# Row maxima in causal attention: four PSUM banks used as a ring, and another pacing of the maxima

## The chip, the cores and the metric

The kernel runs on one core of one Trainium2 chip. The metric is the device time of one execution in microseconds. Three executions of the kernel before took 4935.09, 4936.78 and 4944.33 us; the median is 4936.78.

## What is computed

The program is a whole network of eight stages: a mixture of experts, attention, the mixture of experts again, a channel mix, a state-space layer and a second channel mix. The change touches the attention alone. Its input has 8 batches of 1024 tokens and 256 features; there are 16 heads of 16 features.

```python
logits = jnp.einsum('bhqd,bhkd->bhqk', q, k) * scale
mask = jnp.tril(jnp.ones((T, T), dtype=x.dtype))
logits = logits + (1.0 - mask)[None, None, :, :] * big_neg
attn = jax.nn.softmax(logits, axis=-1)
out = jnp.einsum('bhqk,bhkd->bhqd', attn, v)
```

The kernel computes the softmax as exp(logit - row maximum) over its sum, so every query needs the maximum over its keys before its exponentials are taken.

## The kernel before, in words

`attention` (from line 1006) works on 32 groups, each of four heads of one batch (`GH` = 4, `GROUPS` = 32). It does two things at once on TensorE (PE).

**Maxima.** For head x and query tile j of 128 queries, `maximum` in the tensor program multiplies the 128 queries by the (j + 1) x 128 keys that they may see, in bf16 parts, into PSUM (line 1277, in matmuls of at most 512 columns). VectorE (DVE) adds the causal mask and takes the row maximum in one instruction (line 1229), which also writes a scratch tile, `masked[u % 2]`, and is followed by a read of its accumulator into `mx`. `TILES_M` orders the 32 tiles of a group from large to small: four of 1024 keys, four of 896, and so on to four of 128. When a group's last tile is done, `negated` makes three bf16 parts of the negated maxima (lines 1236 to 1239), `parts` transposes them on PE (line 1284) into PSUM too, `transposed` copies them out (line 1245), and SyncE (SP) puts them as extra rows under the queries (`maxima` in the sync program), so that the score matmul subtracts the maximum by itself. In the order of uses the transposing matmul of a group comes after the first two tiles of the next group (`PARTS_AT` = 2). A reciprocal of an older group's sums (line 1252) comes after tile 24, the first of 256 keys.

**Scores and values.** `score` (line 1301) multiplies keys by queries for a unit, that is a key tile and up to 512 queries. A group has 12 units of 512, 128, 384, 256, 512, 128, 512, 256, 512, 384, 512 and 512 queries (`ORDER`), cut into slots of up to 512 columns, each in one of three banks `psE`: 38 slots a group (`SHARES`). ScalarE (ACT) takes the exponential (line 1213), GpSimd (POOL) zeroes the masked corner of units on the diagonal (line 1192), and two units later `values` (line 1317) multiplies by the values into `psO`, which ACT copies out twice a group (line 1203).

**PSUM.** `psM` is two buffers of two banks each; use u of the maxima takes buffer u % 2, so PE's matmul for use u waits until DVE is through with use u - 2. `psE` has three banks and `psO` one: eight in all.

**Pacing.** PE runs one stream in program order. After each score slot s, `maxima(s)` issues the tiles from `upto[s]` to `upto[s + 1]`. The planner counts a tile at its columns, (j + 1) x 128, and a slot at its score columns, and lets the maxima run `AHEAD` = 1.3 groups ahead of the scores. The first 1.3 groups' tiles are issued before any score, and the last group's slots have few or none left.

Of the kernel before, what the change touches and what calls it, by code (L numbers as in the profile page):

```python
# [18 lines left out]
P = 128  # L19
B, L, D = 8, 1024, 256  # L20
N_TOK = B * L
LT = L // P
DH = D // P
TILES = N_TOK // P
BANK = 512
# [752 lines left out]
GH = 4  # L778
GROUPS = B * NH // GH
HG = NH // GH  # L780
AUG = 2 * HD
PARTS = 3

QREP = (3, 2, 1)
SK = 6 * HD
# [220 lines left out]
def attention(nc, tag, qs, ks, vs, oT, rdd, consts):  # L1006

    with ExitStack() as ctx:
        a = Pool_(nc, ctx, tag)
        identb = a.sb("identb", [P, P], bf16)  # L1010
        later = a.sb("later", [P, L])
        qst = [a.sb(f"qst{u}", [P, GH, L], bf16) for u in range(HG)]
# [4 lines left out]
        masked = [a.sb(f"masked{k}", [P, L]) for k in range(2)]  # L1017
        mx = [a.sb(f"mx{k}", [P, GH * LT]) for k in range(2)]
        mrest = a.sb("mrest", [P, GH * LT])
        mp = a.sb("mp", [P, PARTS, GH * LT], bf16)  # L1020
        mT = a.sb("mT", [PARTS * GH * LT, P], bf16)
# [3 lines left out]
        rden = [a.sb(f"rden{u}", [GH * LT, P]) for u in range(2)]  # L1025
        rd = [a.sb(f"rd{u}", [P, L]) for u in range(2)]
        on = [a.sb(f"on{u}", [P, L]) for u in range(2)]
        psM = [a.ps(f"psM{k}", [P, 2 * BANK]) for k in range(2)]
        NE = 3
        psE = [a.ps(f"psE{k}", [P, BANK]) for k in range(NE)]  # L1030
        psO = a.ps("psO", [P, BANK])
# [2 lines left out]
        m_ready, m_used, mp_ready, m_loaded = (a.sem(n) for n in ("m_ready", "m_used", "mp_ready", "m_loaded"))  # L1034
# [8 lines left out]
        UNITS = [(kt, max(h * BANK, kt * P), (h + 1) * BANK) for h, kt in ORDER]  # L1043
# [20 lines left out]
        uses.update({use_of_parts(g): (g, N_M) for g in range(GROUPS)})  # L1064
        N_USES = len(uses)

        AHEAD = 1.3
        SLOTS = [(n, x, c) for n in range(NU) for x, c in SHARES[n]]
        per_group = sum(GH * (q1 - q0) for _, q0, q1 in UNITS)
        upto, done, k, work = [], 0, 0, 0  # L1070

        def cost(u):
            return (TILES_M[uses[u][1]][1] + 1) * P if uses[u][1] < N_M else 0

        for s in range(-1, GROUPS * NS_):
            if s >= 0:
                n, _, c = SLOTS[s % NS_]
                done += c * (UNITS[n][2] - UNITS[n][1])
            while k < N_USES and work + cost(k) <= done + AHEAD * per_group:
                work += cost(k)  # L1080
                k += 1
            upto.append(k)
# [8 lines left out]
        with nc.Block() as block:  # L1091
# [128 lines left out]
            @block.vector  # L1220
            def _(dve):
                link = Link(dve, d_step)
                dve.wait_ge(consts_loaded, 32)

                def maximum(g, k, u):
                    x, j = TILES_M[k]
                    w = (j + 1) * P
                    dve.wait_ge(m_ready, u + 1)
                    dve.tensor_tensor_reduce(masked[u % 2][:, 0:w], psM[u % 2][:, 0:w], later[:, L - w:], 1.0, -3e38,  # L1229
                                             ALU.add, ALU.max, mx[g % 2][:, x * LT + j:x * LT + j + 1]).then_inc(m_used, 1)  # L1230

                def negated(g, u):
                    m = mx[g % 2]
                    link.at(3 * g)
                    dve.wait_ge(m_used, u + 1)
                    link.step(dve.tensor_scalar(mp[:, 0, :], m[:, :], -1.0, None, ALU.mult))
                    link.step(dve.scalar_tensor_tensor(mrest[:, :], m[:, :], -1.0, mp[:, 0, :], ALU.mult, ALU.subtract))
                    link.step(dve.tensor_copy(mp[:, 1, :], mrest[:, :]))
                    dve.tensor_tensor(mp[:, 2, :], mrest[:, :], mp[:, 1, :], ALU.subtract).then_inc(mp_ready, 1)

                def transposed(g, u):
                    dve.wait_ge(m_ready, u + 1)
                    if g:
                        dve.wait_ge(m_loaded, 16 * PARTS * g)
                    dve.tensor_copy(mT[:, :], psM[u % 2][0:PARTS * GH * LT, 0:P]).then_inc(m_used, 1)

                def inverse(g):
                    u = g % 2
                    dve.wait_ge(den_loaded[u], 16 * GH * (g // 2 + 1))
                    if g >= 2:  # L1250
                        dve.wait_ge(rden_stored[u], 16 * (g // 2))
                    dve.reciprocal(rden[u][:, :], den[u][:, :]).then_inc(r_ready, 1)

                for u in range(N_USES):
                    g, k = uses[u]
                    if k < N_M:
                        maximum(g, k, u)
                        if k == N_M - 1:
                            negated(g, u)
                        if k == INV_AT and g >= 2:  # L1260
                            inverse(g - 2)
                    else:
                        transposed(g, u)
                inverse(GROUPS - 2)
                inverse(GROUPS - 1)

            @block.tensor
            def _(pe):
                def maximum(g, k, u):
                    x, j = TILES_M[k]  # L1270
                    if k == 0:
                        pe.wait_ge(loaded[g % HG], LOADS * (g // HG + 1))
                    if u >= 2:
                        pe.wait_ge(m_used, u - 1)
                    for c in range(0, (j + 1) * P, BANK):
                        r = min(BANK, (j + 1) * P - c)
                        ins = pe.matmul(psM[u % 2][:, c:c + r], qst[g % HG][0:SK, x, j * P:(j + 1) * P],  # L1277
                                        kst[g % HG][0:SK, x, c:c + r], start=True, stop=True)
                    ins.then_inc(m_ready, 1)

                def parts(g, u):
                    pe.wait_ge(mp_ready, g + 1)
                    pe.wait_ge(m_used, u - 1)
                    pe.matmul(psM[u % 2][0:PARTS * GH * LT, 0:P], mp[:, :, :].rearrange("p k n -> p (k n)"),
                              identb[:, :], start=True, stop=True).then_inc(m_ready, 1)

                def maxima(s):
                    for u in range(upto[s], upto[s + 1]) if s >= 0 else range(upto[0]):
                        g, k = uses[u]
                        if k < N_M:  # L1290
                            maximum(g, k, u)
                        else:
                            parts(g, u)

                def score(k, i):
                    g, n = k // NU, k % NU
                    (kt, q0, q1), (x0, c), s = UNITS[n], SHARES[n][i], slots_to(k) + i
                    if s >= NE:
                        pe.wait_ge(w_ready, s - NE + 1)
                    for x in range(c):  # L1300
                        ins = pe.matmul(psE[s % NE][:, x * (q1 - q0):(x + 1) * (q1 - q0)],  # L1301
                                        kst[g % HG][0:SK + PARTS, x0 + x, kt * P:(kt + 1) * P],
                                        qst[g % HG][0:SK + PARTS, x0 + x, q0:q1], start=True, stop=True)
                    ins.then_inc(e_ready, 1)
                    maxima(s)

                def values(k):
                    g, n = k // NU, k % NU
                    kt, q0, q1 = UNITS[n]
                    if n in DIAGS:  # L1310
                        pe.wait_ge(sel_ready, sel_count(g, n))
                    else:
                        pe.wait_ge(w_ready, slots_to(k) + len(SHARES[n]))
                    if n in FIRSTS and k:
                        pe.wait_ge(o_copied, 2 * g + FIRSTS.index(n))
                    for x in range(GH):
                        ins = pe.matmul(psO[AUG * x:AUG * (x + 1), q0 % BANK:q0 % BANK + q1 - q0], va[g % HG][:, kt, x, :],  # L1317
                                        wt[k % NW][:, x, 0:q1 - q0], start=(n in FIRSTS), stop=(n in LASTS))
                    ins.then_inc(w_used, 1)

                LOADS = 16 * (2 * sum(QREP) + 1)
                pe.wait_ge(consts_loaded, 32)
                pe.wait_ge(ones_ready, HG + 2)
                maxima(-1)
                for k in range(GROUPS * NU):
                    if k % NU == 0:
                        pe.wait_ge(m_loaded, 16 * PARTS * (k // NU + 1))
                    shares = SHARES[k % NU]
                    early = (k - LAG) % NU not in FIRSTS
                    for i in range(len(shares)):  # L1330
                        score(k, i)
                        if k >= LAG and i == (len(shares) // 2 if early else len(shares) - 1):
                            values(k - LAG)
                for k in range(GROUPS * NU - LAG, GROUPS * NU):
                    values(k)
# [1412 lines left out]
```

## Time and profile before

| | |
|---|---|
| median of three executions | 4936.78 us |
| the profiled execution | 4933.36 us |
| its span | 4931.6 us |
| PE busy in the span | 4195.4 us (85%) |
| DVE busy | 3070.1 us (62%) |
| ACT busy | 2309.5 us (47%) |
| maxima on DVE, line 1229 | 734.0 us in 1024 instructions |
| maxima on PE, line 1277 | 421.8 us in 1536 matmuls |
| scores on PE, line 1301 | 413.7 us in 1536 matmuls |
| exponentials on ACT, line 1213 | 627.4 us in 1216 instructions |

The first maxima matmul starts at 889.9 us of the span and the last at 1867.7. Times in the profile are microseconds, those marked as a mean are nanoseconds. A matmul's duration contains its drain through the array, so durations of consecutive matmuls overlap; it is the distance of two starts that tells how long one holds the engine. The same holds of DVE and ACT. PEld is the weight load of a matmul.

### The profile page before, as it was taken

How to read it: one execution, taken by the hardware profiler on the slowest of the kernel's cores; microseconds unless marked ns; L12 is line 12 of the kernel's file. 1: busy time of each engine (PE TensorE's matmuls, PEld its weight loads, DVE VectorE, ACT ScalarE, POOL GpSimd, SP SyncE). 2: the span in 40 equal slices, each digit the busy share in tenths (PEclk: the TensorE clock that was granted, in tenths of full speed). 3: DMA queues.
4: the chain of work that ended last, by engine and by line, in shares of the span. 5: the costliest groups of instructions: out<-in, count | busy, mean ns of one | idle time of the engine just before them, and what ended most of it. 6: DMA issues, size and time to landing. Idle time of an engine off the chain costs nothing. (4 is left out here: it accounts for less than half of the span.)

```text
span 4931.6 us, 117903 instructions
## 1 busy us (share of the span) xinstructions
PE 4195.4 (85%) x49696; PEld 2649.1 (54%) x49696; DVE 3070.1 (62%) x5364; ACT 2309.5 (47%) x3824; POOL 2409.9 (49%) x1569
## 2 busy tenths in 40 slices
PE   6399968699999996739997799879999999997798
PEld 5255545233333333625555544367777777875576
DVE  4511145687888884641116466479899899997574
ACT  1021124366666663101115367667667776763233
POOL 1034344222222223113432245479999899997553
PEclk6599989799999998769998899989999999998899
DMA  6132256655555544422323236643333333333552
GB/s 214 39 83 44 37 181 225 110 88 88 88 88 88 88 71 158 144 78 46 49 36 102 85 143 259 233 124 98 94 88 100 94 101 88 98 98 105 215 202 80
DMA packets 325609, 548.93 MB, mean 111 GB/s; under 512 B 55104, under 2 KB 221168, under 8 KB 325072
## 3 DMA queue, kind: packets, MB, share of 16 engines
q1 hardware_dynamic: 291328, 487.10, 36.5%
q0 software_dynamic: 24576, 34.10, 4.4%
q10 hardware_dynamic: 9168, 20.09, 1.1%
q8 instruction: 396, 6.49, 0.6%
q14 instruction: 141, 1.16, 0.1%
HBM read 326.98 MB, written 212.86 MB: 109 GB/s over the span
## 5 line engine op out<-in xcount | busy, mean ns | idle before, releaser
L2331 POOL TENSOR_TENSOR s_hc<-s_hs,s_ct 128x1024 f32<-128x1024 f32 x512 | 1213.5, 2384 | 91.6 <-DVE s_hs L2310 77.1
L2310 DVE TENSOR_TENSOR_SCAN s_hs<-s_dA,s_psB 128x1024 f32<-128x1024 f32 x512 | 1167.3, 2285 | 126.3 <-PE s_psB L2244 63.8
L2244 PE MATMUL s_psB<-s_diag,s_duT 128*32 128x128 f32 x32768 | 962.7, 274 | 53.2 <-issue 28.2
L2244 PEld LDWEIGHTS s_psB<-s_diag,s_duT 128*32 128x32 f32 x32768 | 909.6, 111 | 157.5 <-issue 108.4
L1229 DVE CUSTOM_DVE_ANT_0 a_masked<-a_psM,a_later 128x1024 f32<-128x1024 f32 (+7 forms) x1024 | 734.0, 753 | 213.7 <-PE a_psM L1277 201.5
L1213 ACT ACTIVATE a_wt<-a_psE 128x512 f32<-128x512 f32 (+1 forms) x1216 | 627.4, 578 | 356.1 <-PE a_psE L1301 346.5
L2187 ACT ACTIVATE s_dA<-s_dlt,s_aneg 128x1024 f32<-128x1024 f32 x512 | 587.8, 1148 | 343.5 <-DVE s_hs L2310 339.6
L1192 POOL TENSOR_SCALAR_AFFINE_SELECT a_wt<-a_wt 128x512 f32<-128x512 f32 x256 | 162.3, 634 | 769.9 <-ACT a_wt L1213 769.9
L1277 PE MATMUL a_psM<-a_kst,a_qst 96*128 96x512 bf16 (+3 forms) x1536 | 421.8, 337 | 99.9 <-DVE a_mx L1229 68.0
L1301 PE MATMUL a_psE<-a_qst,a_kst 99*128 99x512 bf16 (+3 forms) x1536 | 413.7, 331 | 4.1 <-ACT a_wt L1213 2.4
L2167 ACT ACTIVATE s_diag<-s_ident,s_bt 128x128 f32<-128x128 f32 x972 | 322.2, 388 | 13.6 <-ACT s_ys L2176 13.5
L1317 PE MATMUL a_psO<-a_wt,a_va 128*32 128x512 f32 (+3 forms) x3072 | 328.1, 499 | 0.4 <-POOL a_wt L1192 0.4
L1301 PEld LDWEIGHTS a_psE<-a_qst,a_kst 99*128 99x128 bf16 x1536 | 129.0, 97 | 325.3 <-ACT a_wt L1213 218.3
L1277 PEld LDWEIGHTS a_psM<-a_kst,a_qst 96*128 96x128 bf16 x1536 | 143.4, 98 | 295.9 <-DVE a_mx L1229 203.2
L2257 PE MATMUL s_psY<-s_hc,s_gsum 128*32 128x512 f32 x2064 | 251.6, 597 | 5.9 <-POOL s_hc L2331 5.9
L1991 PE MATMUL s_ps<-s_hT,s_w_in 128*128 128x512 f32 x512 | 224.7, 597 | 1.7 <-ACT s_hT L1794 1.3
L667 POOL DMA_INDIRECT x<-m2f_y,m_slots x64 | 100.8, 1575 | 216.4 <-DVE m2f_y L711 201.8
L667 POOL DMA_INDIRECT x<-m1f_y,m_slots x64 | 100.8, 1575 | 216.1 <-DVE m1f_y L711 201.5
L691 ACT ACTIVATE m2f_mid<-m2f_psU,m2f_bu 128x512 f32<-128x512 f32 x96 | 65.8, 686 | 282.5 <-PE m2f_psU L744 282.5
L691 ACT ACTIVATE m1f_mid<-m1f_psU,m1f_bu 128x512 f32<-128x512 f32 x96 | 65.8, 686 | 282.4 <-PE m1f_psU L744 282.4
L759 PE MATMUL m1f_psD<-m1f_wdn,m1f_mid 128*128 128x256 f32 (+1 forms) x768 | 190.5, 394 | 0.0
L759 PE MATMUL m2f_psD<-m2f_wdn,m2f_mid 128*128 128x256 f32 (+1 forms) x768 | 190.5, 394 | 0.0
(305 smaller groups left out, 5939.4 us busy)
## 6 DMA issues: line engine op xcount, KB each, us to landing
s_dlt<-dd SPq DMA_DIRECT2D x128, 512.0 KB, 4.5
a_qst<-qs SPq DMA_DIRECT2D x192, 128.0 KB, 6.7
a_kst<-ks SPq DMA_DIRECT2D x192, 128.0 KB, 7.2
yd<-s_ys ACTq DMA_DIRECT2D x33, 512.0 KB, 2.7
vs<-a_va SPq DMA_DIRECT2D x8, 2048.0 KB, 6.9
a_va<-vs SPq DMA_DIRECT2D x32, 512.0 KB, 10.4
zsd<-s_zs SPq DMA_DIRECT2D x32, 512.0 KB, 7.5
ucd<-s_uc SPq DMA_DIRECT2D x8, 2048.0 KB, 13.3
```

The source lines that it names most:

```text
L759: ins = pe.matmul(psD[k][:, j * D:(j + 1) * D], mid[u][0:r, f, t * P:(t + 1) * P], wdn[0:r, e, f, :], start=(f == 0), stop=(f == FT - 1))
L1213: act.activation(wt[k % NW][:, x:x + c, 0:q1 - q0], psE[s % NE][:, 0:c * (q1 - q0)].rearrange("p (x q) -> p x q", x=c), ACT.Exp, scale=HD ...
L1229: dve.tensor_tensor_reduce(masked[u % 2][:, 0:w], psM[u % 2][:, 0:w], later[:, L - w:], 1.0, -3e38, ALU.add, ALU.max, mx[g % 2][:, x * LT ...
L1277: ins = pe.matmul(psM[u % 2][:, c:c + r], qst[g % HG][0:SK, x, j * P:(j + 1) * P], kst[g % HG][0:SK, x, c:c + r], start=True, stop=True)
L1301: ins = pe.matmul(psE[s % NE][:, x * (q1 - q0):(x + 1) * (q1 - q0)], kst[g % HG][0:SK + PARTS, x0 + x, kt * P:(kt + 1) * P], qst[g % HG][0 ...
L1317: ins = pe.matmul(psO[AUG * x:AUG * (x + 1), q0 % BANK:q0 % BANK + q1 - q0], va[g % HG][:, kt, x, :], wt[k % NW][:, x, 0:q1 - q0], start=( ...
L2167: ins = act.activation(diag[:, place(n, u), c, :], ident[:, :], ACT.Copy, scale=bt[u][:, c, n:n + 1])
L2187: act.activation(dA[k % 2][:, :], dlt[j % 2][:, q % NB, :], ACT.Exp, scale=aneg[:, k:k + 1]).then_inc(dA_ready, 1)
L2244: ins = pe.matmul(psB[s][DG * m:DG * (m + 1), c * P:(c + 1) * P], duT[j % 2][:, c, DG * r:DG * (r + 1)], diag[:, place(NB * g + m, u), c, ...
L2257: ins = pe.matmul(psY[DG * r:DG * (r + 1), c:c + BANK], gsum[:, :], hc[NB * (g % 2) + r][:, c:c + BANK], start=(g == 0), stop=(g == NQ - 1))
L2310: dve.tensor_tensor_scan(hs[k % 2][:, :], dA[k % 2][:, :], psB[s][:, :], 0.0, ALU.mult, ALU.add).then_inc(scanned, 1)
L2331: pool.tensor_tensor(hc[NB * (g % 2) + r][:, :], hs[k % 2][:, :], ct[:, g, :], ALU.mult).then_inc(weighed, 1)
```

## The change

`psM` becomes one tensor of four banks, and a planner gives each use a place in it: two neighbouring banks, from an even one, for tiles of 640 keys and more (`TILES_M[..][1] * P >= BANK`), one bank for tiles of up to 512 keys and for the transposing matmul. Places go round the four banks. PE's matmul for use u waits for the last earlier use that held any of its banks (`free[u]`). DVE's instruction for use u waits, besides for the matmul, until use u - 2 is done, whose scratch tile it writes over. The pacing counts a tile at its columns plus 76 (`START`), and scales the slots so that a group's slots weigh as much as a group's tiles.

```diff
-        psM = [a.ps(f"psM{k}", [P, 2 * BANK]) for k in range(2)]
+        psM = a.ps("psM", [P, 4 * BANK])
...
+        place, free, holder, at = [], [], [0] * 4, 0
+        for u in range(N_USES):
+            n = 2 if uses[u][1] < N_M and TILES_M[uses[u][1]][1] * P >= BANK else 1
+            at = (at + n - 1) // n * n % 4
+            place.append(at * BANK)
+            free.append(max(holder[at:at + n]))
+            holder[at:at + n] = [u + 1] * n
+            at += n
+
         AHEAD = 1.3
         SLOTS = [(n, x, c) for n in range(NU) for x, c in SHARES[n]]
-        per_group = sum(GH * (q1 - q0) for _, q0, q1 in UNITS)
+
+        START = 76
+        per_group = sum(j * P + P + START for _, j in TILES_M)
+        columns = sum(GH * (q1 - q0) for _, q0, q1 in UNITS)
         upto, done, k, work = [], 0, 0, 0
 
         def cost(u):
-            return (TILES_M[uses[u][1]][1] + 1) * P if uses[u][1] < N_M else 0
+            return (TILES_M[uses[u][1]][1] + 1) * P + START if uses[u][1] < N_M else 0
 
         for s in range(-1, GROUPS * NS_):
             if s >= 0:
                 n, _, c = SLOTS[s % NS_]
-                done += c * (UNITS[n][2] - UNITS[n][1])
+                done += c * (UNITS[n][2] - UNITS[n][1]) * per_group / columns
...
                 def maximum(g, k, u):
                     x, j = TILES_M[k]
                     w = (j + 1) * P
+                    if u >= 2:
+
+                        dve.wait_ge(m_used, u - 1)
                     dve.wait_ge(m_ready, u + 1)
-                    dve.tensor_tensor_reduce(masked[u % 2][:, 0:w], psM[u % 2][:, 0:w], later[:, L - w:], 1.0, -3e38,
+                    dve.tensor_tensor_reduce(masked[u % 2][:, 0:w], psM[:, place[u]:place[u] + w], later[:, L - w:], 1.0, -3e38,
                                              ALU.add, ALU.max, mx[g % 2][:, x * LT + j:x * LT + j + 1]).then_inc(m_used, 1)
...
-                    if u >= 2:
-                        pe.wait_ge(m_used, u - 1)
+                    if free[u]:
+                        pe.wait_ge(m_used, free[u])
                     for c in range(0, (j + 1) * P, BANK):
                         r = min(BANK, (j + 1) * P - c)
-                        ins = pe.matmul(psM[u % 2][:, c:c + r], qst[g % HG][0:SK, x, j * P:(j + 1) * P],
+                        ins = pe.matmul(psM[:, place[u] + c:place[u] + c + r], qst[g % HG][0:SK, x, j * P:(j + 1) * P],
                                         kst[g % HG][0:SK, x, c:c + r], start=True, stop=True)
                     ins.then_inc(m_ready, 1)
 
                 def parts(g, u):
                     pe.wait_ge(mp_ready, g + 1)
-                    pe.wait_ge(m_used, u - 1)
-                    pe.matmul(psM[u % 2][0:PARTS * GH * LT, 0:P], mp[:, :, :].rearrange("p k n -> p (k n)"),
+                    pe.wait_ge(m_used, free[u])
+                    pe.matmul(psM[0:PARTS * GH * LT, place[u]:place[u] + P], mp[:, :, :].rearrange("p k n -> p (k n)"),
                               identb[:, :], start=True, stop=True).then_inc(m_ready, 1)
```

## Rows read from the trace of the kernel before

**Rows 1.** Stretches: length; busy PE, PEld, DVE, ACT, POOL (count); clock; DMA share; GB/s.

```profile
890.00:920.00 30.00, 24.12 (x57) 4.83 (x55) 26.59 (x74) 0.00 (x0) 0.00 (x0) 0.50 0.80 125
1304.90:1335.58 30.68, 28.52 (x197) 9.36 (x194) 24.71 (x71) 20.59 (x41) 7.82 (x12) 1.00 0.58 89
```

**Rows 2.** Waits, 1000 to 1800 us: who waited for whom, us, times, longest.

```profile
PEld a_psE L1301 <- ACT a_wt L1213: 172.2, 286, 0.8
PEld a_psM L1277 <- DVE a_mx L1229: 151.6, 286, 0.8
DVE a_masked L1229 <- PE a_psM L1277: 144.1, 287, 1.4
```

**Rows 3.** PE in order of time: start us, us, line, tiles, shape, count [idle before].

```profile
1304.91 0.39 PE L1301 MATMUL a_psE<-a_qst,a_kst 99*128 99x512 bf16 x1
...
1305.84 0.38 PE L1301 MATMUL a_psE<-a_qst,a_kst 99*128 99x512 bf16 x1
1306.49 0.39 PE L1277 MATMUL a_psM<-a_kst,a_qst 96*128 96x512 bf16 x1 [0.27 <-DVE a_mx L1229]
...
1307.43 1.06 PE L1317 MATMUL a_psO<-a_wt,a_va 128*32 128x512 f32 x8
1308.43 0.39 PE L1301 MATMUL a_psE<-a_qst,a_kst 99*128 99x256 bf16 x2
...
1315.36 0.23 PE L1277 MATMUL a_psM<-a_kst,a_qst 96*128 96x128 bf16 x1
...
1318.10 0.23 PE L1284 MATMUL a_psM<-a_identb,a_mp 128*96 128x128 bf16 x1
...
1321.00 0.38 PE L1301 MATMUL a_psE<-a_qst,a_kst 99*128 99x512 bf16 x1
1321.62 0.55 PE L1277 MATMUL a_psM<-a_kst,a_qst 96*128 96x512 bf16 x2 [0.24 <-DVE a_mx L1229]
...
1333.03 0.45 PE L1277 MATMUL a_psM<-a_kst,a_qst 96*128 96x512 bf16 x2 [0.35 <-DVE a_mx L1229]
...
1335.58 0.39 PE L1301 MATMUL a_psE<-a_qst,a_kst 99*128 99x512 bf16 x1
```

**Rows 4.** DVE in order of time, same group.

```profile
1305.61 0.82 DVE L1229 CUSTOM_DVE_ANT_0 a_masked<-a_psM,a_later 128x640 f32<-128x640 f32 x1 [0.56 <-PE a_psM L1277]
...
1306.36 0.69 DVE L1229 CUSTOM_DVE_ANT_0 a_masked<-a_psM,a_later 128x512 f32<-128x512 f32 x1
...
1306.97 0.69 DVE L1229 CUSTOM_DVE_ANT_0 a_masked<-a_psM,a_later 128x512 f32<-128x512 f32 x1
...
1312.35 0.94 DVE L1252 RECIPROCAL a_rden<-a_den 32x128 f32<-32x128 f32 x1
1313.21 0.35 DVE L1229 CUSTOM_DVE_ANT_0 a_masked<-a_psM,a_later 128x256 f32<-128x256 f32 x1
...
1315.62 0.29 DVE L1229 CUSTOM_DVE_ANT_0 a_masked<-a_psM,a_later 128x128 f32<-128x128 f32 x1
...
1315.96 0.18 DVE L1236 TENSOR_SCALAR a_mp<-a_mx 128x32 bf16<-128x32 f32 x1
...
1316.72 1.22 DVE L1229 CUSTOM_DVE_ANT_0 a_masked<-a_psM,a_later 128x1024 f32<-128x1024 f32 x1
```

**Rows 5.** ACT, then PE, around a copy of psO: slots 5 and 8.

```profile
1327.72 0.58 ACT L1203 COPY a_oS<-a_psO 128x512 f32<-128x512 f32 x1 [0.47 <-PE a_psO L1317]
1328.20 1.65 ACT L1213 ACTIVATE a_wt<-a_psE 128x384 f32<-128x384 f32 x4
...
1327.59 0.34 PE L1301 MATMUL a_psE<-a_qst,a_kst 99*128 99x384 bf16 x1
...
1328.76 0.34 PE L1301 MATMUL a_psE<-a_qst,a_kst 99*128 99x384 bf16 x1
```

**Rows 6.** DVE in order of time, in the opening.

```profile
907.02 0.69 DVE L1229 CUSTOM_DVE_ANT_0 a_masked<-a_psM,a_later 128x512 f32<-128x512 f32 x1
...
907.80 0.69 DVE L1229 CUSTOM_DVE_ANT_0 a_masked<-a_psM,a_later 128x512 f32<-128x512 f32 x1
```

More of the change, by code:

```diff
@@ L1244, in transposed @@
                         dve.wait_ge(m_loaded, 16 * PARTS * g)
-                    dve.tensor_copy(mT[:, :], psM[u % 2][0:PARTS * GH * LT, 0:P]).then_inc(m_used, 1)
+                    dve.tensor_copy(mT[:, :], psM[0:PARTS * GH * LT, place[u]:place[u] + P]).then_inc(m_used, 1)
                 def inverse(g):
```

## The prediction

> **What bounds it now.** After the page I read the stretches [rows 1]: attention is one of eight stages, and its steady part repeats once for each of its 32 groups. In one such period of 30.68 us PE has 28.52 us of busy time, in which the drain of each matmul is counted, DVE 24.71, ACT 20.59, and the granted clock is 1.00, the 2.4 GHz level. So the share of busy time does not say what bounds; the waits do [rows 2]: DVE waits for PE, and PE's queue waits for DVE at the maxima. Waits on ACT are named for PE's weight loads too, but they end while value matmuls are still streaming. The order of PE shows which wait costs.
>
> PE is in order, so I walked one group matmul by matmul, from the score at 1304.91 to the same slot's at 1335.58, 30.67 us [rows 3]. A 512-column bf16 matmul is followed by the next after 0.22 us, 384, 256 and 128 columns after 0.165, 0.11 and 0.055 in the same proportion. A step of values with 512 columns takes 1.00 us (1307.43 to 1308.43). What lies between two matmuls beyond this is a stall. Scores never stall on ACT by more than 0.1 us. Maxima stall twelve times in a group, each time on DVE: the first at 1305.84 + 0.22 = 1306.06, where the tile starts at 1306.49 (0.43), then 0.17, 0.57, 0.44, 0.14, 0.23, 0.63, 0.16, and 0.18 at 1315.36; these nine are tiles of 128 to 512 keys and make 2.95. Three are at big tiles: 0.20 before the transposing matmul at 1318.10, 0.40 at 1321.62, 0.51 at 1333.03. Sum 4.06 us. PE's own work, with a mode gap of 0.09 us ahead of each of 12 value steps, is therefore 30.67 - 4.06 = 26.6 us. **PE is the bound, and 4.06 us a group is the most that buffers for DVE can give back.**
>
> **DVE's durations** come from starts of neighbours [rows 4]: a 640-key tile holds DVE 0.75 us, one of 512 0.61, so 0.134 per 128 keys and 0.076 fixed: 0.48, 0.345 and 0.21 for 384, 256, 128; 0.88, 1.01 and 1.15 for 768, 896, 1024. The reciprocal takes 0.86, the four steps after a group's last maximum 0.88 beyond that tile's 0.21 (1315.62 to 1316.72), and the copy to mT is short. PE's next use of a buffer starts 0.14 us after DVE's tile has run (1306.36 to 1306.49). DVE needs 4 x 5.43 + 1.74 = 23.5 us a group, less than PE.
>
> **The change, part by part.**
> The ring gives tiles of up to 512 keys (16 of 32) and the transposing matmul one bank each, so up to four are in flight; tiles of 640 and more still take two banks, as before. The weighing moves tiles between score slots. I wrote out PE's order from `upto`, `place` and `free` for a middle group, 38 slots: 1024-key tiles now stand in slots 28, 30, 32, 34 (before 28, 31, 33, 35), 896 in 36, 0, 1, 3, 768 in 4, 6, 8, 10, 640 in 11, 12, 14, 15, 512 in 16 to 19, 384 in 20, 20, 21, 22, 256 in 23, 23, 24, 24, 128 in 25, 25, 25, 26. The transposing matmul follows the second 1024-key tile, in slot 30 (before 31), and lies on the bank of the first. No matmul, tile or DMA is added or taken away.
>
> Replay with the durations above, T = 0 at the score of slot 16:
> - Slots 16 to 19: four scores and four 512-key tiles without a stall (each waits for a tile three or four uses back), 8 x 0.22, then values: next score at T 2.85. Before, 3.52 (0.60 of stalls, and a slightly longer tile).
> - Slots 20 to 32: now DVE sets the pace. The first 384-key tile is ready at 3.43 and starts. 4 x 0.48 to 5.35; four of 256 and the reciprocal 2.24 to 7.60; four of 128 0.85 to 8.44; the four steps to 9.33; 1024 to 10.47; 1024 to 11.62. PE runs ahead by as much as the ring holds and stalls for 0.11 at slot 24, 0.37 at 25, 0.13 at 26, 0.04 at 28, then 0.53 at the transposing matmul and 0.64 at slot 32, whose tile wants the bank of the second 1024-key tile (11.62 + 0.14 = 11.76). Sum 1.82 where 2.55 stood.
> - Slot 32's values to slot 15: PE paces it. The stalls of 0.40 and 0.51 go, since the tiles of 896 and 640 are spaced so that DVE is done, bar 0.06 at slot 12. One stall is new: slots 5 to 8 are 384-column scores with one tile between them instead of two. ACT's copy of psO holds its exponential back, which starts 0.62 us after its score and gives its bank back 0.55 later [rows 5]; slot 8 wants that bank 0.83 after slot 5, so PE stalls 1.17 - 0.83 = 0.34.
> Period: 28.6 us by this walk; by the stalls alone 26.6 + 2.22 = 28.8. I take 28.72, between them: a gain of 1.95 us a group.
>
> The maxima of group g + 1 run beside group g, so 31 of 32 periods gain: 31 x 1.95 = 60.5. The opening, where only maxima run, at a granted clock of 0.50 [rows 1], has DVE idle some 0.17 us at every second small tile, eight times (907.02 to 907.80 for a tile of 0.61 [rows 6]): 1.5 more. The tail has no maxima. The new DVE wait (for the tile two back, whose scratch it writes over) I cost at nothing: it is handled ahead of the instruction, while the previous tile runs. Its bounds: nothing, and 0.12 us, what the first step after the last maximum loses to a wait on the tile directly in front (1315.62 + 0.21 to 1315.96). The tile two back has ended when the previous one starts, which puts it near zero; the shortest cover is 0.21 us. PE's waits are as many as before. Where PE's stalls go, nothing on SP or POOL comes late: mT is copied one slot earlier, which leaves its DMA more room before the next group's scores want it; POOL's selects have two to three slots of slack.
>
> **Sum:** 4933.36 - 62 = 4871.4 against the profiled execution's own time, which lies 3.4 below the median of the runs; for the runs that is 4875.
>
> The clock: through the steady stretch it was granted at 1.00 with these twelve stalls in each group [rows 1, 3]. The Trainium skill (TensorE: Matmul & The Clock Gate, "A second HAM failure mode: psum-queue depth-cycling") tells of a kernel that cycles through PSUM banks and whose short idles made the clock swing. By that rule a ring of banks is at risk, and the time would be rival 5's. The rows show the clock at its upper level through the present idles, and the walk makes these shorter, so I leave it at 1.00.
>
> **Rivals.**
> 1. *The wait bites* (slower). The added wait sits in front of each of DVE's 32 tiles. At 0.12 each, DVE would need 27.3 us a group; in slots 20 to 32, where DVE paces, 14 tiles would lose 1.7 of the 1.95 gained: about 4924. From about 0.15 us a tile on, it is slower than before; at 0.2 the 14 tiles lose 2.8 and the period is 31.5: 31 x 0.8 = 25 over the median, 4962. Against it: the tile waited for has ended. Chance 0.06.
> 2. *Less comes back.* PE's order is rigid, and tiles that collide in the 2-bank part or behind ACT's copy may cost more than the walk shows; with half of the 1.95, 4905. 0.20.
> 3. *Nearly all comes back*, if PE gets so far ahead that DVE never waits and the small stalls merge: 4.06 less 0.5 to 1.2 a group, 4820 to 4845. Against it stands DVE's chain of 8.2 us in slots 20 to 32. 0.10.
> 4. *It does not do what it says*: the stalls cover something else (the m row's DMA, POOL) that then binds, and the time stays within 10 us. 0.04.
> 5. *The clock falls*, because PE's idles come at other places. PE's 26.6 us of work at half the rate add up to 26 us to a group, so three such groups eat the gain; ten give about 5135. The granted 1.00 speaks against it [rows 1]. 0.02. (The skill's rule above would end here.)
>
> **Numbers.** 0.58 for the forecast, 4858 to 4890 (the stall count and the walk differ by 0.2 us a group, and each assumed 0.1 us is 3 us). The range takes in half the gain and part of rival 3: 4842 to 4908. A measurement of this kernel tells 0.2%, 10 us, from no change. Faster by more: forecast, rivals 2 and 3, 0.88. Within: rival 4 and a part of 1, 0.05. Slower: the rest of 1, and 5, 0.07.
>
> **What would show it.** The attention period falls from 30.67 to about 28.7; PE's waits on DVE in slots 16 to 26 nearly vanish but stay at the transposing matmul and the 1024-key tile after it; DVE runs without a gap from the first 384-key tile to the second 1024-key one; PE waits for ACT ahead of the fourth 384-column score behind the copy; everything outside attention keeps its time. Wrong: neighbouring short DVE tiles further apart than 0.21 us (rival 1), a period below 28, or a granted clock under 1.

## The result, and the profile after

| | before | after |
|---|---|---|
| median of four executions each | 4940.12 us (4935.09 to 4944.33) | 4877.77 us (4869.10 to 4879.73) |
| after / before, 95% interval | | 0.9871 [0.9854, 0.9888] |
| the profiled execution, its span | 4933.36, 4931.6 | 4879.73, 4878.0 |
| one attention period (median distance of two mT copies) | 30.67 us | 28.80 us |
| attention, from the first weight load for the maxima to the end of ACT's last copy of psO | 1012.0 us | 949.6 us |
| the rest of the program, worked out from the spans | 3919.6 us | 3928.4 us |

Faster by 62.4 us (4940.12 - 4877.77). The predicted time was 4875.

The attention stretch is shorter by 62.4 us as well, where 62 was forecast. The two profiled executions differ by 53.6 only, since the rest of the program took 8.8 longer in the one of after. 7.3 of these lie in the state-space stage (2112.2 against 2119.5 us), which no edit touches; in the ten traces of this study it took from 2112 to 2119.5 us. Kernels with the ring and kernels with two buffers stand at both ends of this spread, so these 7.3 us are no sign of an effect of the change.

One period of after in the view of stretches, in columns as in [rows 1], where one of before stands:

```profile
890.00:920.00 30.00, 23.80 (x58) 4.59 (x56) 27.31 (x76) 0.00 (x0) 0.00 (x0) 0.50 0.94 130
1261.44:1290.24 28.80, 27.68 (x194) 9.32 (x193) 24.40 (x71) 20.52 (x40) 7.82 (x12) 1.00 0.61 102
```

The engines have the same work in a period that is 1.87 us shorter, and the granted clock is 1.00, the 2.4 GHz level, as before. (PE's busy time counts the drain of each matmul, so it falls from 28.52 to 27.68 us though no matmul is gone.) In the opening DVE is busier than before (27.31 against 26.59 of 30 us).

The waits of after, from 1000 to 1740 us (who waited for whom, us, times, longest), answer to [rows 2], which covers 1000 to 1800:

```profile
PEld a_psE L1318 <- ACT a_wt L1227: 194.4, 333, 0.8
DVE a_masked L1246 <- PE a_psM L1294: 109.3, 207, 1.1
PEld a_psM L1294 <- DVE a_mx L1246: 61.6, 179, 0.9
PE a_psM L1301 <- DVE a_mx L1246: 10.3, 26, 0.5
PE a_psM L1294 <- DVE a_mx L1246: 10.2, 26, 0.4
PE a_psE L1318 <- ACT a_wt L1227: 4.6, 26, 0.2
```

PE's weight loads for the maxima waited 151.6 us on DVE in 800 us before, 5.8 a period, and wait 61.6 in 740 us now, 2.4 a period. The three lines with 26 times are stalls that come once in each period: one at the transposing matmul (L1301), one at the 1024-key tile of slot 32 (L1294), one for ACT at a score (L1318). All three were forecast by name.

PE of after in order of time (start us, us, line, tiles, shape, count [idle before]), one period with the places where it stalls:

```profile
1260.17 0.60 PE L1294 MATMUL a_psM<-a_kst,a_qst 96*128 96x512 bf16 x2
1261.16 0.23 PE L1301 MATMUL a_psM<-a_identb,a_mp 128*96 128x128 bf16 x1 [0.39 <-DVE a_mx L1246]
1261.22 0.60 PE L1318 MATMUL a_psE<-a_qst,a_kst 99*128 99x512 bf16 x2
1262.21 0.61 PE L1294 MATMUL a_psM<-a_kst,a_qst 96*128 96x512 bf16 x2 [0.39 <-DVE a_mx L1246]
...
1271.96 0.33 PE L1318 MATMUL a_psE<-a_qst,a_kst 99*128 99x384 bf16 x1
1272.46 0.34 PE L1318 MATMUL a_psE<-a_qst,a_kst 99*128 99x384 bf16 x1 [0.18 <-ACT a_wt L1227]
...
1279.43 0.38 PE L1294 MATMUL a_psM<-a_kst,a_qst 96*128 96x512 bf16 x1
1279.65 0.38 PE L1318 MATMUL a_psE<-a_qst,a_kst 99*128 99x512 bf16 x1
1279.87 0.38 PE L1294 MATMUL a_psM<-a_kst,a_qst 96*128 96x512 bf16 x1
1280.09 0.38 PE L1318 MATMUL a_psE<-a_qst,a_kst 99*128 99x512 bf16 x1
1280.30 0.38 PE L1294 MATMUL a_psM<-a_kst,a_qst 96*128 96x512 bf16 x1
...
1289.96 0.23 PE L1301 MATMUL a_psM<-a_identb,a_mp 128*96 128x128 bf16 x1 [0.39 <-DVE a_mx L1246]
```

At 1279.43 the 512-key tiles and their scores follow one another every 0.22 us, where [rows 3] has stalls between them. The three stalls that stay are read from starts. The first pair of rows: two matmuls of 512 columns take 2 x 0.22, and the transposing matmul starts 0.99 after the first of them, so 0.55. Slot 32: 1262.21 - 1261.22 - 0.44 = 0.55. The score behind ACT's copy: 1272.46 - 1271.96 - 0.165 = 0.34.

DVE of after in order of time, from the last 640-key tile to the second one of 1024 keys:

```profile
1279.10 0.82 DVE L1246 CUSTOM_DVE_ANT_0 a_masked<-a_psM,a_later 128x640 f32<-128x640 f32 x1
...
1279.96 0.69 DVE L1246 CUSTOM_DVE_ANT_0 a_masked<-a_psM,a_later 128x512 f32<-128x512 f32 x1
...
1282.75 0.56 DVE L1246 CUSTOM_DVE_ANT_0 a_masked<-a_psM,a_later 128x384 f32<-128x384 f32 x1 [0.26 <-PE a_psM L1294]
1283.23 0.55 DVE L1246 CUSTOM_DVE_ANT_0 a_masked<-a_psM,a_later 128x384 f32<-128x384 f32 x1
...
1287.28 0.27 DVE L1246 CUSTOM_DVE_ANT_0 a_masked<-a_psM,a_later 128x128 f32<-128x128 f32 x1
...
1287.48 0.28 DVE L1246 CUSTOM_DVE_ANT_0 a_masked<-a_psM,a_later 128x128 f32<-128x128 f32 x1
...
1288.58 1.23 DVE L1246 CUSTOM_DVE_ANT_0 a_masked<-a_psM,a_later 128x1024 f32<-128x1024 f32 x1
...
1289.73 1.22 DVE L1246 CUSTOM_DVE_ANT_0 a_masked<-a_psM,a_later 128x1024 f32<-128x1024 f32 x1
```

Behind the first 384-key tile at 1282.75 no row up to 1289.73 names an idle time. That is 6.98 us; the walk, the prediction's replay of PE and DVE in order, has 3.43 to 10.47, 7.04. The 128-key tiles are 0.20 to 0.21 apart. So in this stretch the added wait costs DVE nothing. But one distance does not fit the prediction: the matmul of the first 512-key tile starts at 1279.43 and DVE's instruction at 1279.96, with DVE free from 1279.85 on (its 640-key tile starts at 1279.10 and holds it 0.75). That is 0.53 us. In the trace of before the shortest such distance for a last matmul of 512 columns is 0.41.

### The profile page after: what moved, and what is told of

Same layout as the page of the kernel before. It is cut to its first block and busy times, and to the rows that moved or that the text cites. A ratio compares the mean times of both kernels' runs of the same rounds, so it can differ in the third digit from the quotient of the medians.

```text
span 4878.0 us, 118925 instructions
## 1 busy us (share of the span) xinstructions
PE 4177.1 (86%) x49696; PEld 2651.0 (54%) x49696; DVE 3061.0 (63%) x5364; ACT 2309.6 (47%) x3824; POOL 2409.6 (49%) x1569
## 5 line engine op out<-in xcount | busy, mean ns | idle before, releaser
L1294 PE MATMUL a_psM<-a_kst,a_qst 96*128 96x512 bf16 (+3 forms) x1536 | 414.5, 335 | 49.6 <-DMA a_va<-vs 27.5
L1318 PE MATMUL a_psE<-a_qst,a_kst 99*128 99x512 bf16 (+3 forms) x1536 | 411.0, 330 | 8.3 <-ACT a_wt L1227 7.9
L1318 PEld LDWEIGHTS a_psE<-a_qst,a_kst 99*128 99x128 bf16 x1536 | 126.0, 97 | 331.0 <-ACT a_wt L1227 248.5
L1294 PEld LDWEIGHTS a_psM<-a_kst,a_qst 96*128 96x128 bf16 x1536 | 139.8, 98 | 192.9 <-DVE a_mx L1246 96.4
```

What stands on the lines that cost most here:

```text
L1294: ins = pe.matmul(psM[:, place[u] + c:place[u] + c + r], qst[g % HG][0:SK, x, j * P:(j + 1) * P], kst[g % HG][0:SK, x, c:c + r], start=Tru ...
```

## The experiments

The interval beside each time is of its ratio to the kernel before, run on the same chip (medians 4936.74 us in the first four experiments, 4936.98 in the other four).

### 1. The ring alone

```diff
-        START = 76
-        per_group = sum(j * P + P + START for _, j in TILES_M)
-        columns = sum(GH * (q1 - q0) for _, q0, q1 in UNITS)
+        per_group = sum(GH * (q1 - q0) for _, q0, q1 in UNITS)
...
-            return (TILES_M[uses[u][1]][1] + 1) * P + START if uses[u][1] < N_M else 0
+            return (TILES_M[uses[u][1]][1] + 1) * P if uses[u][1] < N_M else 0
...
-                done += c * (UNITS[n][2] - UNITS[n][1]) * per_group / columns
+                done += c * (UNITS[n][2] - UNITS[n][1])
```

> The ring and the VectorE wait, with the old pacing (tiles and slots weighed by columns alone). Theory A (the walk of the prediction, PE in order with stalls on VectorE): the nine small stalls shrink from 2.95 to about 1.1 us a group (0.18 at slot 24, 0.74 at 25, 0.12 at 26), the transposing matmul keeps 0.3, the two big-tile stalls of 0.40 and 0.51 stay; 4.06 falls to 2.3 to 2.4, the period is 28.9 to 29.0 and the time 4880 to 4886 us, so that the ring is nearly the whole gain. Rival B (the two parts add up, pacing takes away the 0.91 of the big tiles and the ring the rest): period 29.6 or more, 4905 us or more.

Measured: 4889.71 us, 0.991 [0.9897, 0.9923]; period 29.29 us, attention 965.8. The ring brings 1.38 of the 1.87 us a period. Rival B's 4905 us is out, but the period is 0.3 above what was expected of the walk, and the time 4 us above its range. The two stalls at big tiles show where most of that comes from:

```profile
1300.64 0.55 PE L1292 MATMUL a_psM<-a_kst,a_qst 96*128 96x512 bf16 x2 [0.35 <-DVE a_mx L1244]
...
1312.16 0.45 PE L1292 MATMUL a_psM<-a_kst,a_qst 96*128 96x512 bf16 x2 [0.46 <-DVE a_mx L1244]
```

By the starts around them they are 0.51 and 0.62 us, where 0.40 and 0.51 were expected to stay as before: 0.11 more each, which is the price of the added wait (experiment 3). The stalls at small tiles make 1.26 where about 1.1 was expected; the added wait was at nothing in that walk too.

### 2. The pacing alone

The opposite edit, made in the kernel before.

```diff
-        per_group = sum(GH * (q1 - q0) for _, q0, q1 in UNITS)
+        START = 76
+        per_group = sum(j * P + P + START for _, j in TILES_M)
+        columns = sum(GH * (q1 - q0) for _, q0, q1 in UNITS)
...
-            return (TILES_M[uses[u][1]][1] + 1) * P if uses[u][1] < N_M else 0
+            return (TILES_M[uses[u][1]][1] + 1) * P + START if uses[u][1] < N_M else 0
...
-                done += c * (UNITS[n][2] - UNITS[n][1])
+                done += c * (UNITS[n][2] - UNITS[n][1]) * per_group / columns
```

> The kernel before with the new pacing alone: two buffers of two banks, no added wait. Theory A: the big-tile stalls go (0.91 us), but with two buffers the small tiles stall as much as before or more (0.28, 0.17, 0.43, 0.49, 1.1, 0.49 at slots 18 to 25), 0.3 comes at the transposing matmul, 0.67 at slot 32 and 0.33 on ACT at slot 8; sum 4.35 against 3.96 by the same walk, period 31.0 to 31.1, time 4946 to 4955 us, slightly slower than before. Rival B (evening out VectorE's load is itself the gain): period 29.7, about 4910 us.

Measured: 4956.92 us, 1.0042 [1.0029, 1.0055]; period 30.92, attention 1030.3. The time is 2 us above theory A's range. The period is 0.25 longer than before, which in 31 periods is 8 us. The rest comes from something that neither theory of this experiment had: four periods of 33.7 us and two of 32.2. The stretches around 1101 us of this kernel, columns as in [rows 1]:

```profile
1094.00:1101.00 7.00, 5.62 (x36) 1.75 (x35) 5.97 (x20) 4.80 (x10) 0.64 (x1) 1.00 1.08 123
1101.40:1108.20 6.80, 6.51 (x29) 1.76 (x29) 3.62 (x18) 1.96 (x5) 0.00 (x0) 0.50 0.56 130
1108.20:1115.00 6.80, 5.96 (x36) 1.78 (x35) 4.86 (x9) 4.36 (x9) 0.63 (x1) 1.00 0.18 42
```

The granted clock falls to 0.50, the 1.2 GHz level, for 6.8 us and comes back. What PE did before it:

```profile
1099.13 0.27 PE L1279 MATMUL a_psM<-a_kst,a_qst 96*128 96x256 bf16 x1
1099.73 0.28 PE L1279 MATMUL a_psM<-a_kst,a_qst 96*128 96x256 bf16 x1 [0.33 <-DVE a_mx L1231]
...
1101.21 0.28 PE L1279 MATMUL a_psM<-a_kst,a_qst 96*128 96x256 bf16 x1 [0.86 <-DVE a_mx L1231]
1101.43 1.93 PE L1319 MATMUL a_psO<-a_wt,a_va 128*32 128x512 f32 x8
```

With two buffers, short tiles set closer together end in one idle time of 0.86 us ahead of the third 256-key tile; the values behind it take 1.93 us, where such a row takes 1.06 in [rows 3]. The idle time of 0.86 us comes in every period, and the clock fell in six of 31, so the idle alone does not say when it falls. The four falls of 6.8 us each begin 0.2 us after the matmul behind that idle time, and they come in every third period (at 1101.4, 1197.0, 1292.6 and 1388.2).

### 3. The added wait alone

In the kernel before, whose scratch needs no such wait:

```diff
+                    if u >= 2:
+                        dve.wait_ge(m_used, u - 1)
                     dve.wait_ge(m_ready, u + 1)
```

> The kernel before with the added VectorE wait (use u waits until use u - 2 is done), where it is implied anyway. Theory A: it costs nothing; neighbouring 128-key tiles stay 0.21 us apart, period 30.67, within 5 us of before. Rival 1 of the prediction (the wait bites): 0.05 us on each tile gives a period of about 31.3 (by the walk with two buffers VectorE is on the path at every second small tile), some 15 to 20 us slower; 0.12 gives 40 us and more.

Measured: 4980.08 us, 1.0085 [1.0072, 1.0098]; period 31.66, attention 1055.0. I had expected nothing, and it costs 43 us: 0.98 a period, and three periods of 35.3 in which the granted clock is 0.50 for 10.2 us. The place to look is a tile for which DVE stands idle. DVE and PE of this kernel in order of time:

```profile
1257.39 0.82 DVE L1231 CUSTOM_DVE_ANT_0 a_masked<-a_psM,a_later 128x640 f32<-128x640 f32 x1 [0.56 <-PE a_psM L1279]
1258.14 0.69 DVE L1231 CUSTOM_DVE_ANT_0 a_masked<-a_psM,a_later 128x512 f32<-128x512 f32 x1
...
1258.82 0.69 DVE L1231 CUSTOM_DVE_ANT_0 a_masked<-a_psM,a_later 128x512 f32<-128x512 f32 x1
```

```profile
1258.28 0.39 PE L1279 MATMUL a_psM<-a_kst,a_qst 96*128 96x512 bf16 x1 [0.38 <-DVE a_mx L1231]
```

From 1258.28 to 1258.82 it is 0.54 us, and DVE was free 0.61 after 1258.14, at 1258.75. Over the steady part the shortest distances from the start of a tile's last matmul to DVE's start, with 128, 256, 384 and 512 columns, are 0.253, 0.307, 0.360 and 0.413 us before, and 0.363, 0.413, 0.470 and 0.523 in after. All four are longer by 0.11. With two buffers a tile is one turn of a circle (matmul, DVE, matmul), so each turn that binds should lose 0.11. Stall by stall this is what the two traces show: of the twelve stalls of the prediction nine are longer by 0.10 to 0.13 us, six of them at tiles of 128 to 512 keys (0.43, 0.57, 0.44, 0.23, 0.63 and 0.18 become 0.54, 0.68, 0.55, 0.33, 0.74 and 0.29), and the three at the transposing matmul and the big tiles (0.20, 0.40 and 0.51 become 0.33, 0.51 and 0.62). The 0.17, 0.14 and 0.16 stay: there DVE takes the tile that PE waits for straight after the one before it, as at 1258.14. Together that is the 0.98 of the period; 31 x 0.98 is 30 us, and the three long periods, 3.6 us longer each, make most of the other 13.

The semaphore records of the traces show what differs. Each DVE tile instruction carries one wait there. The wait written first in the program rides on it; the one written second is a small instruction of its own ahead of it (0.021 us). In after and here the one on its own is the wait for the matmul, the one that ends last, and the tile's instruction comes behind it.

### 4. The transposing matmul one tile later

```diff
-        PARTS_AT = 2
+        PARTS_AT = 3
```

> The changed kernel with PARTS_AT = 3: the transposing matmul comes after the third 1024-key tile instead of the second. Theory A: the stalls of 0.53 at the transposing matmul in slot 30 and 0.64 at slot 32 become 0.08 and 0.71, both in slot 32; the period falls by 0.38 us to 28.4 and the time by 12 us, to 4866. Rival D (the DMA of the maxima is as near to the path as PE): mT is copied about 1.5 us later, so the first score of each group waits for its DMA; then PE waits on the DMA in every group and the time is 4878 or more.

Measured: 4887.48 us, 0.9898 [0.9885, 0.9911]; period 28.94, attention 959.3. Theory A expected 4866, and that did not come. The stalls around the transposing matmul shrink from 1.10 to 0.79 as the walk said, and the period still grows by 0.14, because a new stall of 0.42 us stands ahead of a score. The waits of this kernel, 1000 to 1740 us:

```profile
PEld a_psM L1294 <- DVE a_mx L1246: 41.5, 153, 0.4
PEld a_psE L1318 <- DMA a_qst<-a_mT: 16.4, 26, 1.4
PE a_psM L1301 <- DVE a_mx L1246: 16.3, 26, 0.6
PE a_psE L1318 <- DMA a_qst<-a_mT: 8.8, 26, 1.1
```

The transfer that puts the maxima under the queries now ends too late, 26 times in the stretch, once a period. In after it appears once (0.5 us). This is rival D. The prediction mentioned that mT is copied one slot earlier as a small extra margin; the margin matters, since one tile later this transfer is what PE waits for.

### 5. The two waits the other way round, in after

```diff
+                    dve.wait_ge(m_ready, u + 1)
                     if u >= 2:
-
                         dve.wait_ge(m_used, u - 1)
-                    dve.wait_ge(m_ready, u + 1)
```

> The changed kernel with VectorE's two waits in the other order: first for the matmul, then for use u - 2. Theory E (from the traces so far: the wait that stands first in the program rides on VectorE's instruction, the second becomes an instruction of its own ahead of it; the changed kernel has the wait for PE as the separate one, and its tiles start 0.11 us later behind a matmul, 0.52 against 0.41 for 512 columns): the distance goes back to 0.41, the stalls at slots 12 and 24 fall by 0.1 each, the period from 28.80 to about 28.6, the time by 6 to 7 us. Rival F (the extra instruction itself costs the 0.11, in whatever order): distance 0.52, period 28.80, no change.

Measured: 4870.37 us, 0.9871 [0.985, 0.9892]; period 28.63, attention 944.8, 4.8 us less than after. The shortest distance with 512 columns is 0.414 again. PE and DVE of this kernel:

```profile
1280.91 0.38 PE L1293 MATMUL a_psM<-a_kst,a_qst 96*128 96x512 bf16 x1
```

```profile
1281.33 0.69 DVE L1245 CUSTOM_DVE_ANT_0 a_masked<-a_psM,a_later 128x512 f32<-128x512 f32 x1
```

0.42 us where after has 0.53. The wait for the scratch now stands on its own instruction, has long been fulfilled and is free. The stalls at slots 12 and 24 go from 0.16 and 0.21 to 0.05 and 0.10, as theory E had it. In the whole time the gain is too small for these intervals: the ratio is that of after. The trace carries it.

### 6. The same in the kernel before

```diff
                     dve.wait_ge(m_ready, u + 1)
+                    if u >= 2:
+                        dve.wait_ge(m_used, u - 1)
```

> The kernel before with the added wait, but behind the wait for the matmul in program order. Theory E: nothing of the 43 us of the run with the waits the other way round is left: distance from matmul to VectorE 0.41 us for 512 columns, period 30.67, the granted clock at 1.00 through the steady part, time within 5 us of before. Rival F: distance 0.52, period 31.65, time near 4975 us.

Measured: 4936.49 us, 1.0 [0.9988, 1.0013]; period 30.69, and the granted clock stays at 1.00 through the steady part. Its stalls are those of before to 0.01 us. Experiments 3 and 6 hold the same two waits and differ only in their order: 43 us.

### 7. Tiles of up to 512 keys first

Experiment 5, and the small tiles of a group ahead of the big ones, spread more widely by the pacing.

```diff
-        TILES_M = [(x, j) for j in reversed(range(LT)) for x in range(GH)]
+        TILES_M = [(x, j) for j in (3, 2, 1, 0, 7, 6, 5, 4) for x in range(GH)]
...
-        INV_AT = 24
+        INV_AT = 26
...
-        AHEAD = 1.3
+        AHEAD = 1.37
...
-        START = 76
+        START = 150
```

> The changed kernel with the waits in the other order and another plan: a group's tiles of 512 to 128 keys first, then 1024 to 640, START = 150, AHEAD = 1.37, the reciprocal after tile 26, so that VectorE's dense stretch (small tiles, reciprocal, four steps) is no longer followed by 1024-key tiles in a part where PE has few value steps. The walk with the durations of before gives 1.1 us of stalls a group instead of 2.4 and a period of 27.5 us: 1.3 x 31 = 40 us less than the changed kernel, about 4838 us. If the walk misses a dependence (the reciprocal's or the maxima's DMA), the period stays above 28 us with PE or VectorE waiting for a DMA in every group.

Measured: 4840.63 us, 0.9806 [0.979, 0.9822]; period 27.60, attention 914.4. The walk had 27.5 and 4838. This beats both kernels: 96 us under the kernel before and 30 under experiment 5, which has the same order of waits (4870.37); all three ran on one chip. One period of it:

```profile
1300.00:1327.60 27.60, 27.08 (x195) 9.73 (x195) 24.31 (x71) 20.46 (x41) 7.80 (x12) 1.00 0.61 98
```

The waits of it, 1000 to 1740 us:

```profile
DVE a_masked L1245 <- PE a_psM L1293: 76.8, 161, 1.2
PEld a_psM L1293 <- DVE a_mx L1245: 29.7, 106, 0.4
```

The group's four closing steps now follow a 640-key tile and meet small tiles with four banks to run ahead in, instead of two big tiles that fill the ring. PE's weight loads wait for DVE half as long as in after (29.7 against 61.6 us), and the period is 1.0 above PE's own 26.6. Order, pacing and the place of the reciprocal (`INV_AT`) were changed together; which of them carries the gain wasn't tried.

### 8. Big and small tiles in pairs

Again with the waits in the order of experiment 5.

```diff
-        TILES_M = [(x, j) for j in reversed(range(LT)) for x in range(GH)]
+        BIG, SMALL = ([(x, j) for j in js for x in range(GH)] for js in ((7, 6, 5, 4), (3, 2, 1, 0)))
+        TILES_M = [t for i in range(0, 16, 2) for t in BIG[i:i + 2] + SMALL[i:i + 2]]
...
-        AHEAD = 1.3
+        AHEAD = 1.4
...
-        START = 76
+        START = 150
```

> As the run with small tiles first, but the tiles alternate, two of 640 to 1024 keys and two of 512 to 128, START = 150, AHEAD = 1.4. The walk gives 1.2 us of stalls a group and a period of 27.6 us, about 4841 us. If evenness of VectorE's load were all that counts, this order would be the best; but a pair of one-bank tiles leaves only two banks for the next big one, so that it should not beat the run with small tiles first by more than 3 us.

Measured: 4841.02 us, 0.9802 [0.9785, 0.9819]; period 27.71, attention 921.1. The walk had 27.6 and 4841. Experiments 7 and 8 end at the same time, with orders that have little in common but that the small tiles no longer stand together ahead of the closing steps; their pacing differs a little too.

## Why the prediction was right, point by point

| stall of one period, us | predicted | after |
|---|---|---|
| slot 12 | 0.06 | 0.16 |
| slots 24, 25, 26, 28 | 0.11, 0.37, 0.13, 0.04 | 0.21, 0.28, 0.11, 0.11 |
| transposing matmul (slot 30) | 0.53 | 0.55 |
| slot 32 | 0.64 | 0.55 |
| slot 8, on ACT | 0.34 | 0.34 |
| sum (4.06 before) | 2.22 | 2.31 |

**The bound.** PE's own 26.6 us a period held. With all stalls from 0.03 us up counted in a steady period of each kernel, in us (1 to 8 are the experiments):

| | before | after | 1 | 2 | 3 | 4 | 5 | 6 | 7 | 8 |
|---|---|---|---|---|---|---|---|---|---|---|
| stalls | 4.12 | 2.31 | 2.77 | 4.38 | 5.10 | 2.42 | 2.14 | 4.14 | 1.10 | 1.23 |
| period | 30.67 | 28.80 | 29.29 | 30.92 | 31.66 | 28.94 | 28.63 | 30.69 | 27.60 | 27.71 |
| period less stalls | 26.55 | 26.49 | 26.52 | 26.54 | 26.56 | 26.52 | 26.49 | 26.55 | 26.50 | 26.48 |

So the stalls explain every period, and that is what shows the mechanism: in its steady part, with the clock at 1.00, none of these kernels gained or lost in any other way. (The 4.12 of before counts 0.04 at a score, which the prediction's 4.06 leaves out.)

**The walk.** All stalls named came, none other, and the two of 0.40 and 0.51 went. The stall count gave 28.8 for the period, the walk 28.6, and I took 28.72 between them; the gain was forecast 31 x 0.08 = 2.5 us too large. That the stall count hits 28.80 is luck: it had the added wait at nothing, and the kernel in which this wait costs nothing (experiment 5) has 28.63, which is the walk's figure. In the stall count PE's own work was 0.1 too high and the stalls 0.1 too low.

**The sum.** The 31 distances between mT copies add up to 951.0 us before and 890.8 in after, 60.2 less where 60.5 was forecast. (That is more than 31 x 1.87, chiefly because two periods of before are longer than the others, 31.5 and 31.8.) The maxima ahead of the first copy took 28.6 and 27.8 us, 0.8 less where the opening was to give 1.5 (eight times 0.17 is rather 1.4). What the forecast gave nothing for is the tail behind the last copy: 32.3 and 31.0 us, 1.3 less. That is the clock: before has 3.4 us at 0.50 at 1870.8 us, inside its tail, and after has none until attention ends. Of the other traces with the tiles in this order, experiment 1 has no such fall and a tail of 31.0 too, and experiments 2 to 5, each with 3.4 us at 0.50 in it, have 32.1 to 32.3. The small misses cancel. That the median of the runs lies so near 4875 is partly luck: the state-space stage alone moves by 7 us.

**The added wait was mis-priced.** "The new DVE wait ... I cost at nothing" was the term of the sum that failed. The reasoning asked when the waited-for tile ends, and that was right: neighbouring short tiles are 0.21 apart, and where DVE is behind, the wait is free. It did not ask what the second wait does to the first. Where DVE is idle a tile starts 0.11 us later, just under the upper bound of 0.12 that the prediction gave. After paid 28.80 against 28.63, 0.17 a period, about 5 us: where DVE is idle, the ring mostly keeps PE from needing that tile's bank soon. In two buffers the same edit costs 43 us, more than rival 1's 25. That the time is right in spite of this term is because its price in this kernel is small against 62.

**The split.** The prediction gave one sum for ring and pacing. Alone, the ring gains 1.38 us a period and the pacing loses 0.25; together they gain 1.87. With either kind of buffers the pacing takes the two big-tile stalls away (0.91 us with two buffers, 1.13 with the ring) and puts about as much in their place: the one behind ACT's copy (0.34 in both), the one at slot 32 (0.65 and 0.55) and a little at the transposing matmul and slot 12. The difference lies at the small tiles of slots 16 to 28, which it sets closer together: their stalls stay at 3.0 us with two buffers and fall from 1.26 to 0.71 where the ring lets PE run ahead.

**Rivals.** 1: the wait has a price, but not where the rival put it: it had 14 tiles of slots 20 to 32 lose, where DVE paces, and there they are as close as before; the loss is where DVE is idle. 2: half of the 1.95 was its price; 1.87 came. 3 was wrong for this order of tiles, because of DVE's chain, and experiments 7 and 8, which put the tiles into another order, land in its range (4840.63 and 4841.02). 4 fell. 5 did not happen in after. In the two kernels where the clock fell, experiments 2 and 3, PE idled at other places or longer than before (4.38 and 5.10 us of stalls a period against 4.12). Two of the prices were added up a little wrong: by the prediction's own terms rival 1 at 0.12 comes to 4927 and not 4924, and rival 3 to 4825 to 4847 and not 4820 to 4845. Nothing hangs on it.

The rule of the Trainium skill (TensorE: Matmul & The Clock Gate, "A second HAM failure mode: psum-queue depth-cycling") tells of a kernel that cycles through PSUM banks and whose frequent short idles make the clock swing, and by it the ring would have ended at rival 5's time. The traces do not bear this out for the ring: all six kernels with four banks keep 1.00 in their steady part. The falls came in two of the four two-buffer kernels, those with the most idle time, which agrees with what the page says of idles.

**What stays open.** Why the clock falls in some periods of experiments 2 and 3 and not in others that look the same; how much of the small-tile stalls of experiment 1, 1.26 us against about 1.1, is the added wait; and what moves the state-space stage by 7 us between executions.

## What to carry to other kernels

When an engine works in order and its queue is fixed, walk one period start by start and count only what lies beyond each instruction's own distance: busy shares of 85% and 62% said nothing here, while the period less its stalls was the same to 0.1 us in all ten kernels. When an instruction waits for two things, write first the one that ends last (tried here on DVE alone); the other order cost 43 us in a tight two-buffer circle and about 5 in a ring. Buffers and order are worth trying together: the pacing lost without the ring, and another order of the tiles with its own pacing, once the ring was there, gave another 30 us (experiment 7 against 5).

## What the runs showed of the hardware that I had not expected

- Two waits on one DVE instruction: the one written first stays on it, the later one becomes an instruction ahead of it. If that one ends last and DVE is idle, DVE starts 0.11 us later (0.523 against 0.413 from the start of a 512-column matmul); if it was fulfilled earlier, nothing is lost (0.414).
- The granted clock of PE can fall from 1.00 to 0.50 in the middle of a stretch in which PE is busy 80% of the time (5.62 of 7.00 us), after stalls of up to 0.86 us, and stays there for 6.8 or 10.2 us, a few times for 3.4. A period with a long fall took 33.7 or 35.3 us instead of 30.92 or 31.66.
